# A fused cross-attention and coupling-network kernel on one core: new order at the seam behind the feed-forward stage, and a different order of gelus in its second cycle

## The chip, the cores and the metric

The kernel runs on one core of a Trainium2 chip. The metric is the device time of one execution in microseconds (us), from the first to the last instruction and what lies around them. Five engines work side by side and are tied by semaphores: TensorE (PE; its weight loads stand apart as PEld), VectorE (DVE), ScalarE (ACT), GpSimd (POOL) and SyncE (SP), which issues the DMAs.

## The reference

For each of 64 batches of 256 tokens with 256 features, all in float32:

```
x = x + attention(layernorm(x), ctx, ctx, mask) @ W_out.T
        # 16 heads of 16; logits = tanh(q.k * scale / 4) * exp(log_C); softmax over 120 keys
f = layernorm(x)
gf = sigmoid(global_net(mean of f over tokens))            # three small layers
out = f
for cycle in range(3):
    tf = sigmoid(w4 . gelu(w3 . gelu(w2 . gelu(w1 . out))))   # 256 -> 256 -> 128 -> 64 -> 1, per token
    coupling = 0.1 + adaptive_range * (0.7 gf + 0.3 tf - 0.5) * 2
    out = out + coupling * twist(out)                         # twist permutes and negates quarters
x = x + out
```

The gelu is the exact one; the sigmoids are computed as tanh of half the argument.

## The kernel before

**Stages.** The 64 batches go in 8 groups of 8. `slots()` gives the order that every engine follows: attention slots `i`, and after the slot in which the last batch of a group has its features, the feed-forward stage ("ffn") of that group. In slot `i` the scores of batch `i`, the weighted values of batch `i-1` (`here`), the projection of batch `i-2` (`old`) and the features of batch `i-3` are worked on, and the transposed queries and keys of batch `i+1` (`nxt`) are made. The slot right behind an ffn stage is called `early` on PE; `after_ffn(i)` is true for it. In what follows it is e. There are seven such seams; the eighth ffn stage is the last work before the end of the kernel. Each engine has its own program, written out by hand, and waits on semaphores.

**The ffn stage.** It runs 12 passes p: 3 cycles over 4 chunks of 512 tokens. A pass is a chain over two engines: ACT `gelu1(p)` (L973, two halves), PE `layer2(p)` (L1294), ACT `gelu2(p)` (L997), PE `layer3(p)` (L1303), ACT `gelu3(p)` (L1009). In the first two cycles (p below 8, `UPDATES`) PE `layer4(p)` (L1321), ACT `tanh4(p)` (L1021) and a DVE update of f_t follow: `update_both` for p below 4 (L802, L804, L808, L811, eight instructions), `update_u` for p from 4 to 7 (L824, L827, four instructions). `gelu1(p)` of the later cycles reads what the update of pass p-4 wrote, one half after the other. In the third cycle PE `token_output(p)` (L1334, four small matmuls) follows instead, and after the last of them ACT `token_tanh` (L1027), from which POOL's `coefficients` makes the factors of the residual.

In the loop over p from 5 on, PE's order in a round is layer4(p-2), layer3(p-1), layer2(p) while p is at most 8, and then layer2(p), token_output(p-2), layer3(p-1). ACT's order is tanh4(p-2), gelu3(p-1), gelu2(p), gelu1(p+1) while p is at most 8, and then gelu1(p+1), gelu2(p), gelu3(p-1).

**The seam.** Part of slot e is done inside the ffn stage. PE issues scores(e, 0) in round 10, scores(e, 1) in round 11, weighted_values(e-1, 0) in round 12, token_output(11) in round 13; then in slot e: project(e-2, 0) (L1215), queries(e+1) (L1159), weighted_values(e-1, 1) (L1200), keys(e+1) (L1168), project(e-2, 1), norm_to_features(e-3) (L1228). Slot e+1 begins with scores(e+1, 0) (L1184). ACT issues tanh(e, 0) (L939) in round 10, tanh(e, 1) in round 11 in front of gelu3(11), then token_tanh, exp(e, 0) (L945), features(e-3) (L955), and in the next slot tanh(e+1, 0), exp(e, 1), tanh(e+1, 1).

The token outputs lie in the PSUM bank TR_BANK, which layer3 and the transposes of queries and keys use too. So `queries(e+1)` waits for the token tanh, and `scores(e, 1)` for `tanh(e, 0)`, whose banks it overwrites.

Of the kernel before, what the change touches and what calls it, by code (L numbers as in the profile page):

```python
# [45 lines left out]
def xattn_ffn_kernel(nc, x, ctx, mask, W_out, scale, log_C,  # L46
# [30 lines left out]
    with ExitStack() as stack:  # L77
# [119 lines left out]
        L2_BANKS = (4, 5)  # L197
        L3_BANK = TR_BANK
        SMALL_AT = S
        TOKEN_AT = S + 32  # L200
        L4_BANK = X_BANK
        L4_PAIR = (0, 1)

        def banks(first, n=1):
            return ps_flat[:, first * BANK:(first + n) * BANK]
# [128 lines left out]
        def groups_before(i):  # L334

            return (i - LAG) // GROUP
# [274 lines left out]
        def _(eng):  # L611
# [245 lines left out]
            for kind, i in slots():  # L857
                if i == 2 and kind == "attention":
                    split_weights()
                if kind == "attention":  # L860
                    new, nxt, here, old = ahead_in_slot(i), i + 1, i - 1, i - 2
                    if i == -2:
                        stats(0)
                        attention_constants()
                        stats(1)
                    if 0 <= here < NB:
                        attn_out(here, 0)
                    if 0 <= nxt < NB:
                        queries_out(nxt)
                    if new is not None and 2 <= new < NB:  # L870
                        stats(new)
                    if not after_ffn(i):
                        for b in late[:1]:
                            combine(b)
                    if place(i) in HIGH_AT:
                        high_half((i - LAG) // GROUP, HIGH_AT.index(place(i)))
                    if 0 <= nxt < NB:
                        keys_out(nxt)
                    if place(i) in SIDE_OUT:
                        side_out((i - LAG) // GROUP, SIDE_OUT[place(i)])  # L880
                    if 0 <= here < NB:
                        attn_out(here, 1)
                        divide(here)
                        attn_features(here)
                    if 0 <= old < NB:
                        residual(old)
                        stats_2(old)
                    if after_ffn(i):
                        for b in late[:1]:
                            combine(b)  # L890
                    late = late[1:]
                    if i == 0:
                        weight_constants()
                    if i == 1:
                        largest_weight()
                        coupling_constants()
                else:

                    for m in range(EK):
                        straight_first_out(i, m)  # L900
                    high_half(i, 2)
                    for b in ahead_in_ffn(i):
                        stats(b)
                    high_half(i, 3)
                    eng.wait_ge(s_gact, 3 * (i + 1))
                    eng.wait_ge(s_coef, COEFS * i)
                    eng.tensor_scalar(c_batch[:], gth[:], c_glob[:, 0:1], 0.1, ALU.mult, ALU.add).then_inc(s_gcs, 1)
                    eng.wait_ge(s_gcs, i + 1)
                    eng.wait_ge(s_ct, 5)
                    eng.tensor_scalar(r_batch[:], c_batch[:], ct_inv[:, 0:1], None, ALU.mult).then_inc(s_ratio, 1)  # L910
                    for p in range(CHUNKS):
                        update_both(i, p)
                    for p in range(CHUNKS, UPDATES):
                        update_u(i, p)
                    late = list(range(i * GROUP, (i + 1) * GROUP))
# [15 lines left out]
        def _(eng):  # L931
# [92 lines left out]
            def token_tanh(g):  # L1024
                eng.wait_ge(s_ztok, CHUNKS * (g + 1))
                eng.wait_ge(s_coef, COEFS * g)
                eng.activation(tok_th[:], banks(TR_BANK)[:, TOKEN_AT:TOKEN_AT + GT], ACT.Tanh, scale=0.5,  # L1027
                               bias=half_b4[:, 0:1]).then_inc(s_ttok, 1)

            eng.wait_ge(s_vec0, N_BIAS)  # L1030
            for kind, i in slots():
                if kind == "attention":
# [7 lines left out]
                        tanh(i, 1)  # L1040
                    if 0 <= i < NB:
                        exp(i, 0)
                    if 0 <= i - LAG < NB:
                        features(i - LAG)
                    if last and i < NB:
                        exp(i, 1)
                else:
# [39 lines left out]
                    gelu1(i, 4)  # L1087
                    gelu2(i, 3)
                    straight_out(i, 3, 1)
                    gelu3(i, 3)  # L1090
                    gelu2(i, 4)
                    gelu1(i, 5)
                    for p in range(CHUNKS + 1, PASSES + 1):
                        if p - 2 < UPDATES:
                            tanh4(i, p - 2)
                        if p <= UPDATES:
                            gelu3(i, p - 1)
                            gelu2(i, p)
                            gelu1(i, p + 1)
                        else:  # L1100
                            if p + 1 < PASSES:
                                gelu1(i, p + 1)
                            if p < PASSES:
                                gelu2(i, p)
                            gelu3(i, p - 1)
                            if early < NB and p >= PASSES - 2 and p < PASSES:
                                tanh(early, p - PASSES + 2)
                    token_tanh(i)
            eng.wait_ge(s_coef, COEFS * NGROUPS)
            eng.wait_ge(s_upd, EK * UPDATES * NGROUPS)  # L1110
# [8 lines left out]
        def _(eng):  # L1119
# [26 lines left out]
            def queries(b):  # L1146

                eng.wait_ge(s_qhat, 2 * (b + 1))
                if b == 0:
                    eng.wait_ge(s_vec0, N_BIAS)  # L1150
                elif after_ffn(b - 1):
                    eng.wait_ge(s_ttok, groups_before(b - 1))
                elif b >= LAG + 2:
                    eng.wait_ge(s_ft, 2 * (b - LAG - 1))
                else:
                    eng.wait_ge(s_kt, b)
                for k in range(EK):
                    for t in range(TT):
                        last = eng.transpose(banks(TR_BANK)[:, k * S + t * P:k * S + (t + 1) * P],  # L1159
                                             q_hat[:, b % QR, t, k * P:(k + 1) * P], ident[:])  # L1160
                last.then_inc(s_qtr, 1)
# [43 lines left out]
            def project(b, t):  # L1205
                eng.wait_ge(s_oft, b + 1)
                if t == 0:
                    if b == 0:
                        eng.wait_ge(s_vec0, N_SPREAD)
                    else:  # L1210
                        eng.wait_ge(s_y, b)
                    if after_ffn(b + 2):
                        eng.wait_ge(s_th, UPDATES * groups_before(b + 2))
                for k in range(EK):
                    last = eng.matmul(banks(X_BANK)[:, t * E:(t + 1) * E], of_t[:, k, t * P:(t + 1) * P],  # L1215
                                      wo_t[:, k, :], start=(k == 0), stop=(k == EK - 1))
# [111 lines left out]
            def token_output(g, p):  # L1328
# [1 line left out]
                chunk, n = slot_of(p)[1], PASSES * g + p  # L1330
                eng.wait_ge(s_h3, n + 1)
                for t in range(TT):
                    at = TOKEN_AT + t * GROUP + chunk * CB
                    last = eng.matmul(banks(TR_BANK)[:, at:at + CB], h3[:, p % 2, t * P:(t + 1) * P],  # L1334
                                      w4rep[:, :, 0], start=True, stop=True)
                last.then_inc(s_ztok, 1)

# [16 lines left out]
            for kind, i in slots():  # L1354
                if kind == "attention":
# [3 lines left out]
                    if i != early:  # L1359
# [9 lines left out]
                            scores(i, 1)  # L1369
                        if 0 <= old < NB:  # L1370
                            project(old, 0)
                    else:
                        if old < NB:
                            project(old, 0)
                        if nxt < NB:
                            queries(nxt)
                        if here < NB:
                            weighted_values(here, 1)
                    if 0 <= nxt < NB:
                        keys(nxt)  # L1380
                    if 0 <= here < NB and i != early:
                        weighted_values(here, 1)
                    if 0 <= old < NB:
                        project(old, 1)
                    if 0 <= i - LAG < NB:
                        norm_to_features(i - LAG)
                    if i == 0:
                        transpose_w_out()
                    if i == 1:
                        largest_beside()  # L1390
                else:
# [30 lines left out]
                    for p in range(CHUNKS + 1, PASSES + 2):  # L1422
                        if p - 2 < UPDATES:
                            layer4(i, p - 2)
                        if UPDATES < p < PASSES:
                            layer2(i, p)
                        if p - 2 >= UPDATES:
                            token_output(i, p - 2)
                        if p - 1 < PASSES:
                            layer3(i, p - 1)  # L1430
                        if p <= UPDATES:
                            layer2(i, p)
                        if early < NB:
                            if p == PASSES - 2:
                                scores(early, 0)
                            if p == PASSES - 1:
                                scores(early, 1)
                            if p == PASSES:
                                weighted_values(early - 1, 0)


# [25 lines left out]
```

## Time and profile before

| what | value |
|---|---|
| median of 3 runs | 1058.44 us (1058.36 to 1059.02) |
| the profiled execution's own time | 1058.27 us |
| its span, first to last instruction | 1056.4 us |
| busy: PE, ACT, DVE, POOL | 974.1, 899.3, 818.9, 604.4 us |
| mean granted TensorE clock | 0.981 |

The span is shorter than the time of the same execution by what lies around the instructions. Busy times are sums over a kernel with two kinds of stage; matmul ends are modelled, so a busy PE is not PE at its peak.

### The profile page before, as it was taken

Reading aid. Unit: us, or ns where it says so; the run is one execution under the profiler, and the core shown is the slowest. Engines: PE = TensorE matmul, PEld = TensorE weight load, DVE = VectorE, ACT = ScalarE, POOL = GpSimd, SP = SyncE. Lnnn points to the kernel's source line nnn. Section 1 sums busy time; section 2 is a strip of 40 time slices with the busy share of each in tenths; the row PEclk is TensorE's granted clock in tenths of the full one; section 3 lists DMA queues with packets and bytes.
Section 4 is the critical chain, followed back from the end, with each engine's and each line's share of the span. In section 5 each row is a group of like instructions: output and inputs, shape, how many; then the busy total and the mean of one; then the engine's idle time right before and its main releaser. Section 6 shows DMA issues by size and latency. Waiting matters only on the chain.

```text
span 1056.4 us, 21739 instructions
## 1 busy us (share of the span) xinstructions
PE 974.1 (92%) x7260; PEld 529.3 (50%) x7260; DVE 818.9 (78%) x1655; ACT 899.3 (85%) x1121; POOL 604.4 (57%) x1077
## 2 busy tenths in 40 slices
PE   5899999999999999999999999999999999997993
PEld 4556435564356544565445653556435654454432
DVE  3888785997869876887869978599786887687475
ACT  3899878997899978998789987899789997896575
POOL 3366715887069850898328980588706975087204
PEclk7999999999999999999999999999999999999897
DMA  5433001430023300332005310153002430021002
GB/s 119 89 60 60 6 2 31 118 89 1 2 69 91 78 1 1 90 92 57 2 1 119 89 30 1 30 119 90 0 2 70 94 75 1 1 49 38 11 1 80
DMA packets 191117, 51.70 MB, mean 49 GB/s; under 512 B 165920, under 2 KB 174624, under 8 KB 191008
## 3 DMA queue, kind: packets, MB, share of 16 engines
q1 hardware_dynamic: 191008, 50.31, 22.1%
q8 instruction: 60, 0.98, 0.4%
q14 instruction: 49, 0.40, 0.1%
HBM read 33.37 MB, written 16.78 MB: 47 GB/s over the span
## 4 chain that ended last, share of the span: by engine, by line
PE 46%; ACT 37%; issue 10%; POOL 3%; SPq 2%; DVE 1%; DMA 1%; ACTq 0%; POOLq 0%; DVEq 0%
ACT probs L939 17%; PE ps L1294 15%; ACT probs L945 13%; PE ps L1280 8%; PE ps L1264 6%; PE ps L1303 5%; ACT f_t L955 4%; PE ps L1184 4%; PE ps L1215 3%; PE ps L1200 2%; ACT h L997 1%; PE ps L1324 1%; ACT h L973 1%; PE ps L1334 1%; SPq L412 1%
## 5 line engine op out<-in xcount | busy, mean ns | idle before, releaser
L939 ACT ACTIVATE probs<-ps,u_scale 120x2048 f32<-120x2048 f32 x128 | 258.0, 2015 | 21.2 <-PE ps L1184 20.4
L945 ACT ACTIVATE probs<-probs,exp_bias,clip 120x2048 f32<-120x2048 f32 x128 | 275.6, 2153 | 0.1
L1294 PE MATMUL ps<-h,w 128*128 128x512 f32 x384 | 185.7, 606 | 9.9 <-ACT h L973 8.7
L1184 PE MATMUL ps<-q_t,k_t 32*120 32x256 f32 x2048 | 148.2, 403 | 26.7 <-ACT probs L939 25.9
L717 DVE STREAM_TRANSPOSE o_t<-ps 128x512 f32<-128x512 f32 x128 | 90.6, 708 | 71.5 <-PE ps L1200 71.2
L1215 PE MATMUL ps<-wo_t,of_t 128*128 128x256 f32 x512 | 143.5, 403 | 1.0 <-DVE xy L742 1.0
L498 POOL TENSOR_SCALAR tok_c<-tok_c,c_tok 128x32 f32<-128x32 f32 x8 | 2.3, 288 | 241.6 <-issue 241.6
L1200 PE MATMUL ps<-probs,va 120*32 120x256 f32 x2048 | 138.8, 389 | 1.3 <-ACT probs L945 1.3
L1184 PEld LDWEIGHTS ps<-q_t,k_t 32*120 32x120 f32 x2048 | 93.8, 179 | 63.8 <-issue 59.5
L1215 PEld LDWEIGHTS ps<-wo_t,of_t 128*128 128x128 f32 x512 | 86.9, 189 | 50.0 <-issue 41.7
L1294 PEld LDWEIGHTS ps<-h,w 128*128 128x128 f32 x384 | 67.5, 189 | 87.9 <-issue 58.4
L479 POOL TENSOR_SCALAR f_hat<-xy,neg,rstd 128x256 f32<-128x256 f32 x128 | 102.6, 808 | 13.3 <-POOL rstd L469 13.3
L557 POOL TENSOR_TENSOR f_hl<-f_t,f_hl 128x512 f16<-128x512 f32 x64 | 83.2, 1311 | 35.6 <-DVE f_hl L764 35.6
L973 ACT ACTIVATE h<-f_t,b 128x512 f32<-128x512 f32 x144 | 95.6, 714 | 6.8 <-DVE f_t L827 5.5
L997 ACT ACTIVATE h<-ps,b 128x512 f32<-128x512 f32 x96 | 65.7, 684 | 40.9 <-PE ps L1294 40.9
L458 POOL TENSOR_SCALAR q_hat<-xy,neg,rstd 128x256 f32<-128x256 f32 x128 | 88.1, 696 | 11.0 <-POOL rstd L448 10.5
L1280 PE MATMUL ps<-f_hl,w_hl 128*128 128x512 f16 x384 | 92.6, 385 | 0.0
L802 DVE SCALAR_TENSOR_TENSOR move_u<-coup,r_batch,v_t 128x512 f32<-128x512 f32 x64 | 45.9, 758 | 48.0 <-ACT coup L1021 47.1
L1200 PEld LDWEIGHTS ps<-probs,va 120*32 120x32 f32 x2048 | 53.8, 110 | 56.8 <-ACT probs L945 18.4
L539 POOL TENSOR_SCALAR twisted<-xy,neg,b_r 128x256 f32<-128x256 f32 x112 | 70.5, 637 | 1.2 <-POOL x_add L498 1.1
L1264 PE MATMUL ps<-f_hl,w1t_hl 128*128 128x512 f16 x288 | 68.8, 379 | 0.1
L1303 PE MATMUL ps<-h,w 128*64 128x256 f32 x384 | 62.6, 404 | 3.5
(138 smaller groups left out, 1766.0 us busy)
## 6 DMA issues: line engine op xcount, KB each, us to landing
xy<-in_x_dram SPq DMA_DIRECT2D x64, 256.0 KB, 3.4
out_dram<-xy SPq DMA_DIRECT2D x64, 256.0 KB, 2.0
cbuf<-in_ctx_dram SPq DMA_DIRECT2D x64, 120.0 KB, 2.8
va<-in_ctx_dram SPq DMA_DIRECT2D x64, 120.0 KB, 3.6
tok_c<-coup SPq DMA_DIRECT2D x256, 0.5 KB, 2.0
move_v<-in_L_xattn_W_out_dram SPq DMA_DIRECT2D x1, 256.0 KB, 5.2
move_u<-in_L_ffn_cn_w_dram SPq DMA_DIRECT2D x1, 256.0 KB, 3.3
w<-in_L_ffn_cn_w_dram SPq DMA_DIRECT2D x1, 128.0 KB, 3.1
```

Of the source, the lines that this page charges most:

```text
L479: eng.tensor_scalar(f_hat[:, t, :], xy[:, at, t * E:(t + 1) * E], neg2[:, at, t:t + 1], rstd2[:, at, t:t + 1], ALU.add, ALU.mult).then_inc ...
L717: eng.transpose(o_t[:, b % 2, 2 * n:2 * n + 2].rearrange("p c q r -> p (c q r)"), banks(PV_BANK)).then_inc(s_ot, 1)
L939: eng.activation(probs[:, b % 2, n * HALF:(n + 1) * HALF, :].rearrange("k h q -> k (h q)"), banks(SCORE_BANK, 4)[0:KEYS, :], ACT.Tanh, sca ...
L945: eng.activation(p, p, ACT.Exp, scale=clip[0:KEYS, 0:1], bias=exp_bias[:, b:b + 1]).then_inc(s_exp, 1)
L973: eng.activation(h1[:, p % 2, m, :], source, ACT.Gelu, bias=b1[:, m:m + 1], scale=by) \
L1184: last = eng.matmul(banks(SCORE_BANK + r)[0:KEYS, odd * S:(odd + 1) * S], k_t[rows, b % 2, odd, n, :], q_t[rows, b % 2, n, :], start=True, ...
L1200: last = eng.matmul(banks(PV_BANK)[j * SLOT:(j + 1) * SLOT, (c % 2) * S:(c % 2 + 1) * S], va[:, b % VR, h, :], probs[:, b % 2, h, :], star ...
L1215: last = eng.matmul(banks(X_BANK)[:, t * E:(t + 1) * E], of_t[:, k, t * P:(t + 1) * P], wo_t[:, k, :], start=(k == 0), stop=(k == EK - 1))
L1264: last = eng.matmul(banks(V_BANKS[m]), w1t_hl[:, w, k, m * P:(m + 1) * P], halves[:, f, k, :], start=(n == 0), stop=(n == len(PRODUCTS) - 1))
L1280: last = eng.matmul(banks(U_BANKS[m]), w1_hl[:, w, k, m * P:(m + 1) * P], halves[:, f, k, :], start=(n == 0), stop=(n == len(PRODUCTS) - 1))
L1294: last = eng.matmul(banks(bank), w2[:, k, :], h1[:, p % 2, k, :], start=(k == 0), stop=(k == EK - 1))
L1303: last = eng.matmul(banks(L3_BANK)[b * M3:(b + 1) * M3, 0:S], w3[:], h2[:, p % 2, b * S:(b + 1) * S], start=True, stop=True, tile_position ...
```

## The change

Five edits that belong together:

1. The token outputs move from TR_BANK to X_BANK, where the projection writes. `queries(e+1)` now waits for gelu3(11), `project(e-2, 0)` for the token tanh.
2. PE's order at the seam: scores(e, 1) and weighted_values(e-1, 0) leave the ffn stage. Slot e becomes scores(e, 1), queries(e+1), weighted_values(e-1, 0), keys(e+1), project(e-2, 0), weighted_values(e-1, 1), norm_to_features(e-3), project(e-2, 1). In round 12, layer3(11) goes ahead of token_output(10).
3. ACT: tanh(e, 1) leaves the ffn stage and comes right after exp(e, 0).
4. DVE: in slot e the copy of the queries goes ahead of attn_out(e-1, 0).
5. ACT in the second cycle: in rounds 5 to 8 gelu1(p+1) goes ahead of gelu2(p); the first half of gelu1(5) goes ahead of gelu3(3), the second stays behind gelu2(4).

```diff
@@ DVE, slot @@
+                    if after_ffn(i) and nxt < NB:
+                        queries_out(nxt)
                     if 0 <= here < NB:
                         attn_out(here, 0)
-                    if 0 <= nxt < NB:
+                    if 0 <= nxt < NB and not after_ffn(i):
                         queries_out(nxt)
@@ ACT, token_tanh @@
-                eng.activation(tok_th[:], banks(TR_BANK)[:, TOKEN_AT:TOKEN_AT + GT], ACT.Tanh, scale=0.5,
+                eng.activation(tok_th[:], banks(TOKEN_BANK)[:, 0:GT], ACT.Tanh, scale=0.5,
@@ ACT, slot @@
                         exp(i, 0)
+                    if i < NB and first:
+                        tanh(i, 1)
@@ ACT, ffn stage @@
                     straight_out(i, 3, 1)
+                    gelu1(i, 5, [0])
                     gelu3(i, 3)
                     gelu2(i, 4)
-                    gelu1(i, 5)
+                    gelu1(i, 5, [1])
...
                             gelu3(i, p - 1)
+                            gelu1(i, p + 1)
                             gelu2(i, p)
-                            gelu1(i, p + 1)
...
-                            if early < NB and p >= PASSES - 2 and p < PASSES:
-                                tanh(early, p - PASSES + 2)
+                            if early < NB and p == PASSES - 2:
+                                tanh(early, 0)
@@ PE, waits @@
                 elif after_ffn(b - 1):
-                    eng.wait_ge(s_ttok, groups_before(b - 1))
+                    eng.wait_ge(s_h3, PASSES * groups_before(b - 1))
...
                     if after_ffn(b + 2):
-                        eng.wait_ge(s_th, UPDATES * groups_before(b + 2))
+                        eng.wait_ge(s_ttok, groups_before(b + 2))
@@ PE, slot e @@
                     else:
-                        if old < NB:
-                            project(old, 0)
+                        if i < NB:
+                            scores(i, 1)
                         if nxt < NB:
                             queries(nxt)
                         if here < NB:
+                            weighted_values(here, 0)
+                        if nxt < NB:
+                            keys(nxt)
+                        if old < NB:
+                            project(old, 0)
+                        if here < NB:
                             weighted_values(here, 1)
...
                         norm_to_features(i - LAG)
+                        if old < NB:
+                            project(old, 1)
@@ PE, ffn stage @@
-                        if p - 2 >= UPDATES:
+                        if p - 2 >= UPDATES and p < PASSES:
                             token_output(i, p - 2)
                         if p - 1 < PASSES:
                             layer3(i, p - 1)
+                        if p >= PASSES:
+                            token_output(i, p - 2)
                         if p <= UPDATES:
                             layer2(i, p)
-                        if early < NB:
-                            if p == PASSES - 2:
-                                scores(early, 0)
-                            if p == PASSES - 1:
-                                scores(early, 1)
-                            if p == PASSES:
-                                weighted_values(early - 1, 0)
+                        if early < NB and p == PASSES - 2:
+                            scores(early, 0)
```

## Rows read from the trace of the kernel before

**Rows 1.** Head of the profile page and its chain that ended last, by engine.
```profile
span 1056.4 us, 21739 instructions
...
PE 46%; ACT 37%; issue 10%; POOL 3%; SPq 2%; DVE 1%; DMA 1%; ACTq 0%; POOLq 0%; DVEq 0%
```

**Rows 2.** Timeline of ACT, ffn stage 2: start, us, what, idle before and its releaser.
```profile
268.10 0.47 ACT L1009 ACTIVATE h<-ps,b 128x256 f32<-128x256 f32 x1 [0.96 <-PE ps L1303]
...
269.04 1.33 ACT L973 ACTIVATE h<-f_t,b 128x512 f32<-128x512 f32 x2
270.27 0.68 ACT L1021 ACTIVATE coup<-ps,half_b 128x512 f32<-128x512 f32 x1
...
278.77 0.69 ACT L997 ACTIVATE h<-ps,b 128x512 f32<-128x512 f32 x1 [0.58 <-PE ps L1294]
...
287.76 1.34 ACT L973 ACTIVATE h<-f_t,b 128x512 f32<-128x512 f32 x2 [0.72 <-DVE f_t L827]
```

**Rows 3.** Timeline of DVE, the same stage.
```profile
268.97 1.41 DVE L811 SCALAR_TENSOR_TENSOR v_t<-move_v,ct_neg,v_t 128x512 f32<-128x512 f32 x2
270.98 1.41 DVE L802 SCALAR_TENSOR_TENSOR move_u<-coup,r_batch,v_t 128x512 f32<-128x512 f32 x2 [0.60 <-ACT coup L1021]
...
277.93 1.41 DVE L827 SCALAR_TENSOR_TENSOR f_t<-move_u,ct_safe,f_t 128x512 f32<-128x512 f32 x2
```

**Rows 4.** Timeline of PE, the same stage.
```profile
268.62 0.70 PE L1321 MATMUL ps<-h,w4rep 64*128 64x256 f32 x4 [0.57 <-ACT h L1009]
...
276.77 1.96 PE L1294 MATMUL ps<-h,w 128*128 128x512 f32 x4
278.66 0.70 PE L1321 MATMUL ps<-h,w4rep 64*128 64x256 f32 x4
279.51 0.65 PE L1303 MATMUL ps<-h,w 128*64 128x256 f32 x4
...
283.64 1.95 PE L1294 MATMUL ps<-h,w 128*128 128x512 f32 x4 [0.85 <-ACT h L973]
```

**Rows 5.** Timeline of PE, from round 11 of stage 2 over its seam.
```profile
292.27 0.65 PE L1303 MATMUL ps<-h,w 128*64 128x256 f32 x4
...
296.44 0.61 PE L1334 MATMUL ps<-w4rep,h 128*128 128x2 f32 x4 [0.33 <-ACT h L1009]
...
298.38 1.07 PE L1200 MATMUL ps<-probs,va 120*32 120x256 f32 x16
299.39 0.43 PE L1168 MATMUL ps<-ident,cbuf 120*128 120x120 f32 x2
...
301.22 1.14 PE L1184 MATMUL ps<-q_t,k_t 32*120 32x256 f32 x16
```

**Rows 6.** Timeline of ACT over the same seam.
```profile
290.15 1.97 ACT L939 ACTIVATE probs<-ps,u_scale 120x2048 f32<-120x2048 f32 x1
...
294.06 1.97 ACT L939 ACTIVATE probs<-ps,u_scale 120x2048 f32<-120x2048 f32 x1 [0.61 <-PE ps L1184]
295.92 0.47 ACT L1009 ACTIVATE h<-ps,b 128x256 f32<-128x256 f32 x1
297.08 0.27 ACT L1027 ACTIVATE tok_th<-ps,half_b 128x16 f32<-128x16 f32 x1 [0.70 <-PE ps L1334]
297.38 1.28 ACT L945 ACT_TABLE_LOAD   x1
298.67 2.10 ACT L945 ACTIVATE probs<-probs,exp_bias,clip 120x2048 f32<-120x2048 f32 x1
301.32 0.38 ACT L955 ACTIVATE f_t<-ps 128x256 f32<-128x256 f32 x1 [0.55 <-PE ps L1228]
...
302.42 1.97 ACT L939 ACTIVATE probs<-ps,u_scale 120x2048 f32<-120x2048 f32 x1 [0.26 <-PE ps L1184]
```

**Rows 7.** Timeline of PE in the last ffn stage, which no attention follows.
```profile
1037.74 0.65 PE L1303 MATMUL ps<-h,w 128*64 128x256 f32 x4
```

**Rows 8.** Timeline of ACT in the last ffn stage.
```profile
1040.20 0.47 ACT L1009 ACTIVATE h<-ps,b 128x256 f32<-128x256 f32 x1 [1.29 <-PE ps L1303]
```

More of the change, by code:

```diff
@@ L199, in xattn_ffn_kernel @@
         SMALL_AT = S
-        TOKEN_AT = S + 32
+        TOKEN_BANK = X_BANK
         L4_BANK = X_BANK
@@ L1332, in token_output @@
                 for t in range(TT):
-                    at = TOKEN_AT + t * GROUP + chunk * CB
-                    last = eng.matmul(banks(TR_BANK)[:, at:at + CB], h3[:, p % 2, t * P:(t + 1) * P],
+                    at = t * GROUP + chunk * CB
+                    last = eng.matmul(banks(TOKEN_BANK)[:, at:at + CB], h3[:, p % 2, t * P:(t + 1) * P],
                                       w4rep[:, :, 0], start=True, stop=True)
@@ L1371, in _ @@
                             project(old, 0)
-                    else:
-                        if old < NB:
-                            project(old, 0)
+                        if 0 <= nxt < NB:
+                            keys(nxt)
+                        if 0 <= here < NB:
+                            weighted_values(here, 1)
+                        if 0 <= old < NB:
+                            project(old, 1)
+                        if 0 <= i - LAG < NB:
+                            norm_to_features(i - LAG)
+                    else:
+                        if i < NB:
+                            scores(i, 1)
                         if nxt < NB:
@@ L1377, in _ @@
                         if here < NB:
-                            weighted_values(here, 1)
[L1379 to L1385, printed above, removed]
+                            weighted_values(here, 0)
+                        if nxt < NB:
+                            keys(nxt)
+                        if old < NB:
+                            project(old, 0)
+                        if here < NB:
+                            weighted_values(here, 1)
                         norm_to_features(i - LAG)
+                        if old < NB:
+                            project(old, 1)
                     if i == 0:
```

## The prediction

> **What bounds the kernel now.** I read the page first. The chain that ended last goes 46% over PE and 37% over ACT [rows 1]: the two take turns, and neither DVE nor POOL carries it. So the order of steps on PE and ACT is what can move the time, and only where one of them stands waiting. Then I read the timelines of PE, ACT and DVE over ffn stage 2 and the seam behind it; the other six seams show the same waits within a few hundredths, stage 4 with one DVE pause more.
>
> In the attention slots away from the seam ACT runs without a gap, so whatever tanh(e+1, 0) gains or loses at the seam stays until the next ffn stage. That start, 302.42, is the mark by which I measure. In front of it ACT waited 0.26 for the scores, and PE ran without a stop from 296.44 [rows 5, 6]. At the seam PE is the bound: ACT waits 0.61, 0.70, 0.55 and 0.26 for it [rows 6].
>
> In the second cycle a round takes 3.43 us: layer2(p) ends, gelu2(p) runs, layer3(p) follows, then layer2(p+1). ACT has 0.58 to spare in each [rows 2]. DVE runs its updates back to back from 270.98 on, and gelu1(11) waits 0.72 for the last of them at 287.76 [rows 2, 3]. PE stands 0.85 in front of layer2(9), which waits for gelu1(9), because gelu1(9) is queued behind gelu2(8) [rows 4].
>
> **The gelus of the second cycle (edit 5).** Nothing is added or removed; every instruction keeps its size, and no DMA moves.
>
> The first half of gelu1(5) goes into the 0.96 in which ACT waits for layer3(3) [rows 2], at a cost of nothing: it takes half of the pair, some 0.61 from start to start (269.04 to 270.27 for two). If that gap were gone it would cost those 0.61. tanh4(3) then starts at 270.27 - 0.61 = 269.66; its matmul ended at 268.62 + 0.70 = 269.32, so nothing else holds it [rows 2, 4]. DVE was free at 268.97 + 1.41 = 270.38 and waited until 270.98. It now starts at 270.38: the whole update chain gains 0.60 [rows 3].
>
> What is queued behind gelu1(p+1) is gelu2(p), for which layer3(p) and with it PE wait. gelu1(7) needs update 3 (second half done at about 274.65 in the new schedule), ends its slot at about 275.3 and lets gelu2(6) start in time, at 275.33. gelu1(8) needs update 4: its second half was done at 277.93 + 1.41 = 279.34 and is done at 278.75 now [rows 3]. The second half of gelu1(8) runs from 278.80, and gelu2(7) starts at 279.41 instead of 278.77 [rows 2]: 0.64 late. layer3(7) slips from 279.51 to 280.15, and layer2(8) and layer4(7) with it [rows 4]. gelu1(9) needs update 5, done at 281.74 now, and is through at 282.5, before layer4(7) ends. So layer2(9) follows layer4(7) at once, at 283.37, where it had started at 283.64 after a pause of 0.85 [rows 4]. The slip of 0.64 is eaten by the 0.85, and the stage is 0.27 ahead (the rest are hundredths between modelled ends). From there PE has no gap up to layer3(10): 292.27 becomes 292.00. gelu1(10) and gelu1(11), at 284.8 and 287.2, are in time, the latter because its 0.72 wait shrinks by the 0.60 of the chain.
>
> **The end of the stage (edits 2 and 3).** gelu3(10) ends 0.05 + 0.65 + 0.47 after layer3(10) starts, at 293.17. Nothing is left between it and layer3(11), since the scores and the tanh that lay there are gone: layer3(11) 293.22 to 293.87, gelu3(11) 293.92 to 294.39 instead of from 295.92. token_output(10) fits in behind layer3(11), and token_output(11) starts at 294.44 instead of 296.44 [rows 5, 6]. The token tanh comes 2.00 earlier.
>
> That is no gain yet, as two steps now lie behind it. Before, from token_output(11) to scores(e+1, 0) PE needed 301.22 - 296.44 = 4.78. Now scores(e, 1), 1.14, and weighted_values(e-1, 0), 1.01 from start to start (298.38 to 299.39), are added: 6.93. scores(e+1, 0) starts at 294.44 + 6.93 = 301.37 instead of 301.22 [rows 5]. Term: +0.15 a seam. The work of PE is the same; it lost the scores as cover for gelu3(10) and gelu3(11), and has won 0.27 in the second cycle.
>
> ACT: token tanh, load, exp(e, 0) at 298.67 - 2.00 = 296.67, 2.10 long; tanh(e, 1) 1.97; features 0.84 (301.32 to 302.42 less 0.26) [rows 6]. They end at 301.6 at the latest. norm_to_features ends before them, at about 300.5. ACT then waits some 0.9 for the scores: with tanh(e, 1) moved behind exp, ACT fills a time in which it would have stood anyway. It costs nothing as long as PE needs longer; if PE were faster, ACT would be the bound from 301.6.
>
> The table load: each seam has one in front of the exp, 1.28 long, and exp starts 0.01 behind it [rows 6]. tanh(e, 1) behind the exp brings no second one, as tanh and exp alternate without a load in all slots. The Trainium skill ("ScalarE: Activation LUTs", What ACT_TABLE_LOAD costs) puts a switch of set at about 2.66 us, 1.28 of load and 1.38 of drain. By that ACT would be ready at 303.0, later than the scores, and the seam would lose some 0.5 more. By the trace it is 1.28.
>
> **Bank, waits, DVE (edits 1 and 4).** queries(e+1) no longer waits for the token tanh; it comes behind scores(e, 1), when gelu3(11) is long done. project(e-2, 0) waits for a token tanh that ended at 295.4, some 2.5 before its turn. The copy of the queries comes before attn_out(e-1, 0) on DVE, which it delays by nothing since its matmuls come later anyway; keys(e+1) finds the copy done. I price both at 0. POOL's coefficients start 2.0 earlier; behind them are only the residual parts, for which nobody on the chain waits. SP's queue is untouched. If one of these waits did come last it would cost at most what it exceeds PE's turn by, and I take 0 to 0.3 a seam for the range.
>
> **The last stage.** No scores are in the way there. layer3(10) at 1037.74 - 0.27 = 1037.47 [rows 7]; gelu3(10) ends 1.17 later at 1038.64; layer3(11) to 1039.34; gelu3(11) at 1039.38 instead of 1040.20 [rows 8], as token_output(10) no longer lies between. All that follows hangs on it: -0.82.
>
> **Sum.** 7 x 0.15 - 0.82 = +0.2. The span goes from 1056.4 to 1056.6; with the 1.87 around it (1058.27 less 1056.4) 1058.5. The profiled execution lies 0.17 under the median of the runs, so 1058.6 on their scale. The measurement tells about 0.2%, 2.1 us, from no change: 0.3 a seam. My steps are good to some 0.2 a seam, so this one's own range is 1056.8 to 1060.6.
>
> **Rivals.**
>
> (a) As above: within 0.2%. 0.47.
>
> (b) Slower: DVE does not start update 3 earlier, say because tanh4(3) is held by something I don't see. Then gelu1(7) and gelu1(8), now in front of the gelu2 that PE waits for, stay held by the updates 0.60 longer, and PE with them: 8 x 0.60 = +4.8, 1063.4. For it: DVE runs without slack [rows 3], and every hundredth of it goes on to PE in the new order, as it did not before. Stage 4's pause shows that it can be longer. Against it: 0.96 is enough room for 0.68. It decides from the point at which tanh4(3) starts after 269.7. 0.13.
>
> (c) Slower: the 0.27 of the second cycle isn't won, or PE's steps at the seam don't pack as tightly. The seam alone costs 0.15 + 0.27 = 0.42: 7 x 0.42 - 0.55 = +2.4, 1060.8; with 0.3 a seam for a late wait 1062.9. 0.14. By the drain that the Trainium skill (same section) states it would be 0.5 a seam, +3.7 in all, 1062.1; every load here contradicts it: 0.01, which makes 0.15 with (c).
>
> (d) Faster: ACT sets the seam, not PE. The token tanh comes 2.00 earlier and ACT is ready at 301.6 where it started at 302.42. If the scores were there by then: -0.8 a seam, 7 x -0.8 - 0.8 = -6.4, 1052.0. Against it: 6.93 of PE work in a row, every step seen in the rows. 0.05.
>
> (e) Faster by less: PE gains more than 0.27 in the second cycle (up to the whole 0.85 if gelu1(8) doesn't hold gelu2(7)). Then 7 x (0.15 - 0.58) - 0.82 - 0.58 = -4.4, 1054.0; the half of it 1056.2. For it: the gain of DVE might be larger than 0.60. 0.20.
>
> Chances: faster (d, e) 0.25, same 0.47, slower (b, c and the drain) 0.28. The range of 8 in 10: from the full case (e) to the late wait of (c), 1054.0 to 1062.9.
>
> **What would show it.** ACT: first half of gelu1(5) in front of gelu3(3), tanh4(3) 0.6 earlier. DVE: no wait in front of update 3. PE: a new idle of about 0.8 in front of layer3(7), released by gelu2; the 0.85 in front of layer2(9) gone; a new idle of about 0.6 in front of layer3(11). The token tanh 2.0 earlier. ACT: a wait of about 0.9 for the scores in front of tanh(e+1, 0). The forecast is wrong if gelu2(7) isn't held, if ACT doesn't wait in front of tanh(e+1, 0), or if more than one round is held by DVE.

## The result and the profile after

The changed kernel took 1062.32 us (median of 6 runs, 1061.3 to 1063.24), the kernel before 1058.73 (6 runs, 1057.3 to 1059.67). The ratio is 1.0031 with a 95% interval of 1.0021 to 1.0040: slower by 3.3 us, just over what the measurement can tell from no change. The forecast was 1058.6, no change. On another chip the same two kernels stood at 1.0072 (1.0059 to 1.0085), so the loss is not one number.

The head of the page after, and its chain by engine and by line:

```profile
span 1059.5 us, 21747 instructions
...
PE 43%; ACT 35%; issue 9%; DVE 8%; POOL 3%; SPq 2%; DMA 0%; ACTq 0%; DVEq 0%; POOLq 0%
```

Against [rows 1] DVE has come onto the chain, from 1% to 8%. Those are the steps L802, L804 and L808 of the last updates of the first cycle, in stage 2 from 264.70 to 274.0: gelu1(7) now waits 0.42 for them, and behind it gelu2(6) and PE. gelu1(8) waits 0.96 for the update that follows. In the timeline of ACT after, stage 2 (this stage begins 0.10 earlier than in the trace of before, so that 0.10 has to be added to a time here before it is held against one there or against the forecast):

```profile
266.91 0.74 ACT L975 ACTIVATE h<-f_t,b 128x512 f32<-128x512 f32 x1
268.00 0.47 ACT L1011 ACTIVATE h<-ps,b 128x256 f32<-128x256 f32 x1 [0.35 <-PE ps L1308]
...
269.56 0.69 ACT L1023 ACTIVATE coup<-ps,half_b 128x512 f32<-128x512 f32 x1
...
274.10 1.33 ACT L975 ACTIVATE h<-f_t,b 128x512 f32<-128x512 f32 x2 [0.42 <-DVE f_t L808]
275.34 0.67 ACT L999 ACTIVATE h<-ps,b 128x512 f32<-128x512 f32 x1
...
278.20 1.33 ACT L975 ACTIVATE h<-f_t,b 128x512 f32<-128x512 f32 x2 [0.96 <-DVE f_t L827]
279.44 0.67 ACT L999 ACTIVATE h<-ps,b 128x512 f32<-128x512 f32 x1
```

and in that of PE:

```profile
280.16 0.65 PE L1308 MATMUL ps<-h,w 128*64 128x256 f32 x4 [0.90 <-ACT h L999]
280.74 1.98 PE L1299 MATMUL ps<-h,w 128*128 128x512 f32 x4
...
283.29 1.98 PE L1299 MATMUL ps<-h,w 128*128 128x512 f32 x4
```

Nearly everything here stands where the prediction put it. Half of gelu1(5) is in the gap. With the 0.10 added, tanh4(3) starts 0.61 earlier, as forecast, gelu2(7) at 279.54 (forecast 279.41) and layer2(9) at 283.39 (283.37). layer3(7) has a new idle of 0.90 in front of it, and the 0.85 in front of layer2(9) is gone [rows 4]. Two things are off by about a tenth. DVE starts update 3 at 270.42, 0.13 after it is free, so its chain is 0.47 ahead and not 0.60. And gelu2(6), which was to start in time at 275.33, starts at 275.44: a second round is held by DVE, by 0.11. The seam of stage 2, first PE, then ACT:

```profile
293.22 0.65 PE L1308 MATMUL ps<-h,w 128*64 128x256 f32 x4 [0.62 <-issue]
293.80 1.24 PE L1339 MATMUL ps<-w4rep,h 128*128 128x2 f32 x8
294.97 1.14 PE L1189 MATMUL ps<-q_t,k_t 32*120 32x256 f32 x16
...
301.31 1.14 PE L1189 MATMUL ps<-q_t,k_t 32*120 32x256 f32 x16
```

```profile
295.08 0.27 ACT L1029 ACTIVATE tok_th<-ps,half_b 128x16 f32<-128x16 f32 x1 [0.70 <-PE ps L1339]
295.37 1.28 ACT L947 ACT_TABLE_LOAD   x1
296.67 2.10 ACT L947 ACTIVATE probs<-probs,exp_bias,clip 120x2048 f32<-120x2048 f32 x1
...
302.52 1.97 ACT L941 ACTIVATE probs<-ps,u_scale 120x2048 f32<-120x2048 f32 x1 [1.13 <-PE ps L1189]
```

The token tanh comes 2.00 earlier [rows 6], 1.90 with the 0.10 of the start, and tanh(e+1, 0), the mark, at 302.52 against 302.42. With the 0.10 of the start that is 0.2 lost in this stage and seam. Five of the seven are like that, 7.44 us from the token tanh to the mark. The other two took 9.01 and 8.93. This is seam 5 on PE:

```profile
671.92 2.01 PE L1189 MATMUL ps<-q_t,k_t 32*120 32x256 f32 x16
673.86 1.11 PE L1164 MATMUL ps<-ident,q_hat 128*128 128x128 f32 x4
674.91 1.31 PE L1205 MATMUL ps<-probs,va 120*32 120x256 f32 x16
```

The same scores took 1.14 at seam 2. The windows of seam 5, before the fall and in it (the length, then for each of five engines the busy time and the number of instructions, PE first; the number behind them is the granted clock as a share):

```profile
668.90:671.90 3.00, 2.35 (x17) 1.46 (x16) 0.00 (x0) 1.40 (x3) 0.00 (x0) 1.00 0.00 0
671.90:675.20 3.30, 3.30 (x25) 2.06 (x29) 0.18 (x1) 3.14 (x3) 2.45 (x10) 0.52 0.00 0
```

PE's granted clock is 1.00 (2.4 GHz) up to 671.9, and half (1.2 GHz) for some 3 us behind it. Before the fall PE was busy for 2.35 of 3.00 us, and 8 of its 17 matmuls there are token outputs of 2 columns each. The kernel before has a granted clock of 1.00 at all of its seams. In the 3 us in front of its token tanh PE is busy for 2.67, with scores and weighted values between the token outputs. This is its seam 5:

```profile
670.40:673.40 3.00, 2.67 (x29) 1.61 (x29) 0.72 (x1) 2.30 (x3) 0.00 (x0) 1.00 0.00 0
```

**Where the 3.0 us went.** The last token tanh moved from 1041.78 to 1044.79. The pieces, each a difference of marks between the two traces: up to the first ffn stage -0.27; the five stages with a clean seam +0.18, +0.19, +0.20, +0.27 and +0.20; the two with a fall +1.77 and +1.69; the first matmuls of the last ffn stage -0.35; the rest of that stage -0.87. Together 3.01. Of the 1.77 and 1.69 the falls are 9.01 - 7.44 = 1.57 and 8.93 - 7.44 = 1.49, together 3.06, and 0.20 each is left, as in the clean stages. So the falls are as large as the whole loss, and the rest sums to about 0.

That the rest is so near 0 is in part luck, again of the clock. PE stands idle for 3.92 us in front of the last ffn stage in both kernels, and its granted clock is at half, 0.50, when the stage's first matmuls begin. In the two traces, before and after:

```profile
979.37 4.32 PE L1280 MATMUL ps<-f_hl,w_hl 128*128 128x512 f16 x12
```

```profile
983.60 3.98 PE L1285 MATMUL ps<-f_hl,w_hl 128*128 128x512 f16 x12
```

After, the clock is back 3.3 us behind the start of PE's work, before 4.1 us behind it; this is the -0.35, for the work there is the same in both kernels. The clock falls once more in front of the last token tanh: from layer3(11) to the token tanh it takes 2.28 before and 2.11 after, where it is 1.88 and 1.86 in runs whose clock is full there (edit 5 alone, and the changed kernel again). That is 0.40 and 0.25 for the clock, and 0.15 of the -0.87. The -0.27 ahead of the first ffn stage is not explained.

### The profile page after: what moved, and what is told of

Read it like the earlier page. It is cut to its first block, busy times and chain, and to the rows that moved or that the text cites. A ratio compares the mean times of both kernels' runs of the same rounds, so it can differ in the third digit from the quotient of the medians.

```text
span 1059.5 us, 21747 instructions
## 1 busy us (share of the span) xinstructions
PE 975.0 (92%) x7260; PEld 531.4 (50%) x7260; DVE 820.1 (77%) x1655; ACT 902.5 (85%) x1121; POOL 599.9 (57%) x1077
## 4 chain that ended last, share of the span: by engine, by line
PE 43%; ACT 35%; issue 9%; DVE 8%; POOL 3%; SPq 2%; DMA 0%; ACTq 0%; DVEq 0%; POOLq 0%
ACT probs L941 17%; ACT probs L947 12%; PE ps L1299 11%; PE ps L1285 8%; PE ps L1269 6%; PE ps L1308 4%; PE ps L1189 4%; ACT f_t L957 4%; PE ps L1220 3%; PE ps L1205 3%; DVE move_u L802 2%; DVE move_v L804 2%; DVE f_t L808 2%; PE ps L1339 1%; PE ps L1329 1%
## 5 line engine op out<-in xcount | busy, mean ns | idle before, releaser
L703 DVE COPY q_t<-ps 128x512 f32<-128x512 f32 x64 | 42.2, 659 | 69.5 <-PE ps L1164 69.4
L802 DVE SCALAR_TENSOR_TENSOR move_u<-coup,r_batch,v_t 128x512 f32<-128x512 f32 x64 | 46.1, 762 | 43.8 <-ACT coup L1023 41.9
```

## The experiments

Two theories stood against each other. **Clock theory**: the order costs what the rows gave, and the surplus is the clock that falls at some seams, because PE has little to do in rounds 11 to 13 once scores and weighted values are gone from there. **Order theory**: the surplus comes from the order of steps, the gelus that wait for DVE or the seam, in every execution alike. Every run below was timed against the kernel before on its own chip.

**The changed kernel again.** No edit.

> The changed kernel once more, as the yardstick for the others. Clock theory: the order of the seam costs what the rows of before gave (0.15 to 0.20 us a seam), and each seam at which PE's granted clock falls to half costs 1.5 us more; the number of such seams (2 of 7 in the profile at hand) may differ from execution to execution, so that times lie in steps of about 1.5 us, and the kernel is 2.5 to 4.5 us slower than before. Rival, order theory: the cost is in the order of the steps itself, the same in every execution, 3.3 us slower with no steps in the times.

1065.58 us (1064.54 to 1067.47, 5 runs), ratio 1.0072. Its profile has three seams with a fall, at 10.37, 8.98 and 9.00 instead of 7.44, and they are seams 4, 5 and 6, where the first profile had 5 and 7. Less the 6.0 us of the falls it is 1059.5, which is 1.4 over the 1058.19 of the kernel before on this chip. About as much, 1.3, lies between the two profiles of this same kernel already at the first mark (178.13 against 176.83), ahead of any fall. The windows of its seam 4:

```profile
544.60:547.80 3.20, 2.55 (x17) 1.65 (x16) 0.00 (x0) 1.38 (x3) 0.00 (x0) 0.93 0.00 0
547.80:554.00 6.20, 6.20 (x41) 3.62 (x41) 1.83 (x3) 5.50 (x4) 5.36 (x15) 0.50 0.00 0
```

Here the low level lasted over 6 us and cost 2.9. So there are two sizes of a fall, and where it strikes isn't fixed by the code. The "steps of 1.5 us" that I expected show only roughly, and a loss of 7.4 us is more than the 2.5 to 4.5 that I expected.

**Edits 1 to 4 alone.**

```diff
-                    gelu1(i, 5, [0])
                     gelu3(i, 3)
                     gelu2(i, 4)
-                    gelu1(i, 5, [1])
+                    gelu1(i, 5)
...
-                            gelu1(i, p + 1)
                             gelu2(i, p)
+                            gelu1(i, p + 1)
```

> Edits 1 to 4 alone, the second cycle's gelus in the order of before. Clock theory: PE arrives 0.27 us later at each seam than in the changed kernel, so 0.15 + 0.27 = 0.42 a seam, 7 x 0.42 - 0.55 = +2.4, plus 1.5 us for each seam with a fall, of which there are some here too: +2.4 to +7. Order theory, with the cost in the gelus: the same time as before or faster.

1066.29 us (1061.7 to 1071.0, 6 runs), ratio 1.0078 (1.0052 to 1.0103). Its profile has falls at seams 5 and 6, 10.38 and 9.01. The loss of 8.1 is above the +2.4 to +7 that I expected. The spread of 9.3 us within one kernel fits a number of falls that differs from execution to execution, and the mean granted clock of each run goes with its time: 0.980 at 1061.70 and 1062.61, 0.975 at 1066.27 and 1066.31, 0.971 and 0.972 at 1071.00 and 1070.83. The profiled execution less its 4.5 is 1061.8, 1.0 above the 1060.8 of the forecast for the order alone. From the first mark to the seventh, where the start has no part, it takes 2.47 more than before without its falls, 0.41 a stage; forecast 0.42. The new seam by itself brings the falls.

**Edit 5 alone.**

```diff
+                    gelu1(i, 5, [0])
                     gelu3(i, 3)
                     gelu2(i, 4)
-                    gelu1(i, 5)
+                    gelu1(i, 5, [1])
...
+                            gelu1(i, p + 1)
                             gelu2(i, p)
-                            gelu1(i, p + 1)
```

> Edit 5 alone, the seam in the order of before. Clock theory: no fall at any of the seven seams, layer2(9) 0.27 us earlier in each of 8 stages, so -2.0 to -2.4 us against before, 1056.4. Order theory, with the cost in the gelus that wait for DVE: 1 to 5 us slower than before.

1056.44 us (1055.01 to 1057.01, 11 runs), ratio 0.9981 (0.9972 to 0.9989), that is -2.0 us, as expected; all seven seams of its profile took the 5.33 or 5.34 of before. From the first mark to the seventh it is 1.57 faster, 0.26 a stage, 0.19 to 0.42 in the single ones. So the gelus that wait for DVE gain. The order theory in that form is out.

**A matmul in the gap.** One line on PE, in round 11 behind layer3:

```diff
+                        if early < NB and p == PASSES - 1:
+                            eng.matmul(banks(PV_BANK), ident[:], wo_t[:].rearrange("p k e -> p (k e)"),
+                                       start=True, stop=True)
```

> The changed kernel with one more matmul of 128x512 on PE behind layer3(10), in the 0.62 us in which PE waits for gelu3(10); it writes a bank that nobody reads before it is overwritten. It adds 0.49 us of PE work in a gap of 0.62, so nothing on the path. Clock theory: with that work in the lean stretch no seam has a fall, and the time is 3.0 us under the changed kernel's profile, within 0.5 us of before; if the falls stay, the stretch is still too lean, and only their number tells. Order theory: no change against the changed kernel.

1061.28 us (1060.32 to 1062.31, 7 runs), ratio 1.0027, against 1.0072 of the changed kernel on the same chip. No seam had a fall, all at 7.43 to 7.45. But the time did not come back to within 0.5 us of before, as I had expected; it is 3.1 above the 1058.19. The matmul took 1.05 from start to start, not 0.49: a float32 matmul of 512 columns shows in the trace as two. layer3(11) came 1.64 after layer3(10) and not 1.28, and from mark to mark a stage took some 0.36 more than the clean ones of the changed kernel, 2.5 us in all (the expectation of the next run gives 0.43 for it). I had read the price off layer2, which shows 4 matmuls for what the code writes as 2.

**The same, half the size.**

```diff
-                            eng.matmul(banks(PV_BANK), ident[:], wo_t[:].rearrange("p k e -> p (k e)"),
+                            eng.matmul(banks(PV_BANK)[:, 0:S], ident[:], wo_t[:, 0, :],
```

> The changed kernel with one more matmul of half the size (128x256) behind layer3(10). The 128x512 one took 1.05 us, twice what I had put in (float32 takes two passes), and pushed layer3(11) by 0.43 at each of seven seams; this one should take 0.5 and fit into the gap of 0.62. Clock theory: no or fewer falls, each seam 7.44 us from the token tanh to tanh(e+1, 0), and the time of the changed kernel without its falls, within 0.7 us of before. If a fall remains somewhere, it costs 1.5 us and the stretch is still lean enough. Order theory: 3 us or more over before, with every seam at 7.44.

1059.19 us (1057.96 to 1059.9, 11 runs) against 1059.01, ratio 1.0001 (0.9992 to 1.0010). PE in its trace:

```profile
293.46 0.65 PE L1308 MATMUL ps<-h,w 128*64 128x256 f32 x4
294.04 0.70 PE L1446 MATMUL ps<-wo_t,ident 128*128 128x256 f32 x2
294.74 0.65 PE L1308 MATMUL ps<-h,w 128*64 128x256 f32 x4
295.32 1.24 PE L1339 MATMUL ps<-w4rep,h 128*128 128x2 f32 x8
```

and the windows of its seam 5, to be read against the 2.35 and 0.52 above:

```profile
670.40:673.40 3.00, 2.97 (x21) 1.74 (x21) 0.00 (x0) 1.36 (x3) 0.00 (x0) 1.00 0.00 0
673.40:676.70 3.30, 3.30 (x41) 2.15 (x41) 1.21 (x2) 3.17 (x3) 2.48 (x10) 1.00 0.00 0
```

layer3(11) follows layer3(10) by 1.28, as without the matmul (293.22 - 291.94). All seven seams took 7.43 to 7.46. Useless work that changes no step of the order takes the loss away: it was the clock. The "two passes" of the expectation are the two records in the trace; what the array does in each no run here shows. This is also the only direct measurement of what the forecast was for, the order without the clock: +0.1 us (-0.8 to +1.1), forecast +0.2.

**The scores back in round 11.**

```diff
                         if early < NB and p == PASSES - 2:
                             scores(early, 0)
+                        if early < NB and p == PASSES - 1:
+                            scores(early, 1)
...
                     else:
-                        if i < NB:
-                            scores(i, 1)
                         if nxt < NB:
```

> The changed kernel with scores(e, 1) back in round 11 behind layer3(10), in PE's 0.62 us gap; tanh(e, 1) stays behind exp(e, 0) on ACT. By the rows: layer3(11) starts 0.45 us later (behind scores of 1.07 instead of behind a gap of 0.62), token_output(11) too, and 1.07 of scores are gone behind it, so scores(e+1, 0) comes 0.6 us earlier a seam, to where ACT is ready. Against before 7 x (0.2 - 0.6) - 0.9 = -3.7, 1055.0. Clock theory: no fall at any seam, as PE is filled. Order theory without the clock: 4.2 us under the changed kernel, that is 1058; with falls that come anyway, the same number of them as in the changed kernel.

1057.10 us (1056.76 to 1058.41, 11 runs), ratio 0.9986 (0.9978 to 0.9995): -1.5 us, no fall. The clock part held; of the 3.7 of gain only 1.5 came. The token tanh came 0.4 later and the whole seam took 6.88, where I had reckoned 6.4. PE stood waiting:

```profile
299.59 1.03 PE L1220 MATMUL ps<-wo_t,of_t 128*128 128x256 f32 x4
301.16 1.14 PE L1189 MATMUL ps<-q_t,k_t 32*120 32x256 f32 x16 [0.55 <-ACT probs L941]
```

scores(e+1, 0) overwrites the banks from which tanh(e, 1) reads, and that tanh ends only 5.5 us behind the token tanh, since edit 3 put it behind the exp. The changed kernel has the same dependence, but there tanh(e, 1) ends at 300.62 in stage 2 and PE gets to these scores only at 301.31, so it did not wait.

**gelu1(8) behind gelu2(7).**

```diff
                             gelu3(i, p - 1)
-                            gelu1(i, p + 1)
-                            gelu2(i, p)
+                            if p == 7:
+                                gelu2(i, p)
+                                gelu1(i, p + 1)
+                            else:
+                                gelu1(i, p + 1)
+                                gelu2(i, p)
```

> The changed kernel with gelu1(8) behind gelu2(7), as in before; the other gelu1 stay in front. By the rows gelu2(7) is no longer held by DVE's update 4 and comes 0.64 us earlier, layer3(7) and layer2(8) with it; gelu1(9) waits for update 5 at 281.8 and lets gelu2(8) and PE go on 0.3 to 0.6 earlier than in the changed kernel. 8 x -0.3 to -0.6 = -2.4 to -4.8 us against the changed kernel, if ACT at the seam isn't the bound, with the same kind of falls at the seams. If the hold of gelu2(7) is not on PE's path: no difference.

1060.22 us (11 runs, the lowest 1057.0; one execution of 5267.5 us stands out and has no explanation here), ratio 1.0011 (1.0000 to 1.0021). The profiled execution, 1061.78, has falls at five seams of seven, 7.6 us of them; without them it would be 1054.2, where the two profiled executions of the changed kernel without theirs would be 1058.2 and 1059.5. From mark 3 to mark 4, where neither kernel has a fall, it took 125.19 against 125.89. The gain, 0.70 a stage, is a little larger than the 0.3 to 0.6 expected, and the clock ate most of it.

**Both.** The scores back, and gelu1(8) behind gelu2(7).

> Both: scores(e, 1) back in round 11, and gelu1(8) behind gelu2(7). If the two gains add: 1055.0 less 2.4 to 4.8, 1050.2 to 1052.6, no fall at any seam. If ACT is the bound at the seam once the scores are back, the second still counts, since the token path itself comes earlier.

1052.26 us (1051.33 to 1053.88, 5 runs), ratio 0.9944 (0.9930 to 0.9957), -5.9 us, no fall. The two add: against the run with the scores back, on the same chip, it is 1057.10 to 1052.26, and in the profiles 0.66 a stage. With PE filled at the seam the gain of the gelus is there in full.

**tanh(e, 1) in front of exp(e, 0).** The kernel above, and on ACT:

```diff
+                    if i < NB and first:
+                        tanh(i, 1)
                     if 0 <= i < NB:
                         exp(i, 0)
-                    if i < NB and first:
-                        tanh(i, 1)
```

> The combination of before (scores(e, 1) in round 11, gelu1(8) behind gelu2(7)), and on ACT tanh(e, 1) in front of exp(e, 0) instead of behind it. In the combination scores(e+1, 0) waits 0.54 for tanh(e, 1), whose banks it overwrites, and ACT then 0.61 for the scores. With tanh(e, 1) first it is read out 2.0 us earlier; the scores start when PE is through, 0.55 earlier, and ACT starts tanh(e+1, 0) when its features are done: 0.55 a seam, 7 x -0.55 = -3.9 against 1052.3, 1048.4. If the weighted values of e, which need exp(e, 0), come last in its place, the gain is smaller or nil.

1048.66 us (1047.42 to 1049.07, 4 runs), ratio 0.9902 (0.9887 to 0.9917): 1% faster than before, the best of all, and near the 1048.4 expected. ACT in its trace, from the token tanh to the mark without a wait:

```profile
293.71 0.27 ACT L1029 ACTIVATE tok_th<-ps,half_b 128x16 f32<-128x16 f32 x1 [0.70 <-PE ps L1343]
293.89 1.97 ACT L941 ACTIVATE probs<-ps,u_scale 120x2048 f32<-120x2048 f32 x1
295.87 1.28 ACT L947 ACT_TABLE_LOAD   x1
297.17 2.10 ACT L947 ACTIVATE probs<-probs,exp_bias,clip 120x2048 f32<-120x2048 f32 x1
...
299.99 1.97 ACT L941 ACTIVATE probs<-ps,u_scale 120x2048 f32<-120x2048 f32 x1
```

The seam takes 6.28, 0.60 less than the 6.88 of the kernel above, at each of seven.

## Where the prediction was right and where it was wrong, point by point

The times of the single steps came out to within some 0.2 us. But no change was forecast, and it became 3.3 us slower, by a mechanism that was none of the rivals. That 1062.32 lies inside the range, by 0.6, is luck: its upper end is the late wait of (c), which did not come about, and the 1065.58 of the same kernel on the other chip lies outside.

**The gelus of the second cycle: right in the mechanism, off by a tenth in sizes.** DVE's chain came 0.47 earlier (forecast 0.60), gelu2(7) was held by 0.77 (0.64), gelu2(6) by 0.11 (nothing), and the slip was eaten by the idle of 0.85. In stage 2 layer3(10) is 0.23 ahead (0.27), and the run of edit 5 alone gave -2.0 us, 8 stages of 0.25. One sign of being wrong was that more than one round is held by DVE; it showed, but at 0.11. The hold of gelu2(7) costs somewhat more than the 0.58 by which rival (e) valued it: the runs that take it away won 0.66 and 0.70 a stage. Rival (b), an update 3 that does not start earlier, came about only by the 0.13 that are missing from the 0.60.

**The seam: right in its times.** +0.15 was forecast from mark to mark and 0.18 to 0.27 measured, the 0.27 in the stage with DVE's pause. Token tanh 1.90 earlier (forecast 2.00), ACT's wait for the scores 1.13 (forecast about 0.9). The table load has nothing behind it, 296.67 - 296.65 = 0.02, so the drain by which the seam would have lost more is not there.

**"PE lost the scores as cover": the step that failed.** In that sentence the cover was priced as time only: 0.15 a seam, because PE's work is the same in sum. It didn't look at how thin PE's work gets where the cover was. PE then has an idle of 0.62 and eight matmuls of 2 columns in a row, and at two seams of seven the clock fell to half, 1.57 and 1.49 us each. In the trace of before the clock is 1.00 at each seam, and I took it as given in the new order. The same trace holds a hint: in the last stage, whose end has no attention work between the token outputs, the granted clock falls, from about 1040.6 on, after two idles of 0.57 on PE. The windows of before there:

```profile
1035.00:1038.00 3.00, 3.00 (x14) 1.58 (x16) 0.00 (x0) 2.07 (x5) 1.63 (x8) 1.00 0.02 0
1038.00:1042.00 4.00, 2.59 (x16) 1.65 (x12) 0.00 (x0) 1.36 (x4) 0.00 (x0) 0.82 0.00 0
```

The new seam makes all the others more like that one. The Trainium skill ("TensorE: Matmul & The Clock Gate", What's actually happening) describes a gate with two levels that follows how busy PE has lately been and that doesn't start anew with the kernel. The traces agree: read in steps of 0.25 us the falls show only 1.00 and 0.50, with a value between them where the level changes, and they hit seams 5 and 7 in one execution and 4, 5 and 6 in another of the same kernel. That description was reason enough to make such a fall a rival with a chance of its own; whether it would strike could not be worked out from it.

**The last stage: right, with some luck.** -0.82 forecast, -0.87 measured; of that 0.15 is the clock, which also falls there before the change, and -0.72 the order.

**Sum.** Forecast +0.2 from the order. In the marks it is 1.44 in seven stages, where 1.05 was forecast, and -0.72 in the last: +0.7. The clock of the last stage gave back 0.35 and 0.15, and 0.27 had been won ahead of the first; so the rest without the falls is about 0. The run with the half-size matmul says +0.1 (-0.8 to +1.1). The falls cost 3.1 in the profile and 6.0 on the other chip.

Why a given seam falls and the next doesn't stays open. In the 3 us in front of the token tanh PE is busy for 2.35 at every seam of the four profiles with falls, whether the clock falls there or not, and no run here shows what else decides it.

## What to carry to other kernels

When work moves off an engine's lean stretch, price two things: the time it covered, and the activity that it gave to PE there. Look for a place in the old trace where PE already has the thin pattern, and read its granted clock. A cheap test of a suspected clock loss is one useless matmul in the gap, sized to fit in it; if the time comes back with no step moved, the clock was it, and real work put there is better still.

An order is worth judging by the wait that is second. Here tanh(e, 1) behind the exp cost nothing as long as PE was later still. With the scores in the gap it held PE, and putting it in front gave 0.60 a seam, 4.2 us in seven (1052.26 to 1048.66 between the medians, on two chips).

## What the runs showed that I had not expected

The granted clock fell to half at 2, 3, 2 and 5 of seven seams in four profiles with the lean stretch, for some 3 us at a cost of 1.5, or over 6 us at a cost of 2.9. It fell at none of 35 in the five profiles in which PE had one more matmul, of 0.70 or 1.05 us, or the scores, behind layer3(10) instead of the idle of 0.62; there PE is busy for 2.96 or 2.97 of the 3 us in front of the token tanh. A kernel with such falls can also spread more: 9.3 us over 6 runs with edits 1 to 4 alone, though only 1.9 over 6 in the first measurement of the changed kernel, against 1.9 over 11 with the half-size matmul.

A float32 matmul written as 128x512 takes 1.05 us of PE from start to start, and one of 128x256 takes 0.70 with the modelled end.
